# Pair counts of a graph kernel: one-hots compared two tiles side by side, against lane numbers kept in a PSUM bank

## The reference

```
edge_index = stack([src, dst])                       # 400,000 edges, sorted by dst
x = layernorm(x + L0(x, edge_index, ...))            # attention over the edges, softmax by src
x = layernorm(x + L1(x, node_vec1, ...))             # two masked sums over the edges
x = layernorm(x + L2(x, edge_weight, edge_attr, ...))# radial weights, messages, sum by dst
x = layernorm(x + L3(x, edge_index, ...))            # two graph convolutions
```

## Time and profile before

| | |
|---|---|
| median of 3 runs | 20,091.51 us (20,090.82 to 20,093.43) |
| profiled execution, span from the first to the last instruction | 25,995.0 us |
| time outside the span | none is given |
| busy in the span | PE 9,853; PEld 7,351; DVE 16,714; ACT 6,289; POOL 13,430 us |
| mean granted PE clock | 0.611 of 2.4 GHz |
| pair counts, first comparison to the copy of bank 0 | 1401.9 to 2067.9 us of the span |

### The profile page before, as it was taken

One profiled execution on the slowest core, in us unless ns is written; L12 is line 12 of the kernel. 1 busy time (PEld: TensorE's weight loads), 2 busy tenths in 40 slices (PEclk: granted clock), 3 DMA queues, 4 the chain that ended last, 5 costly groups with the idle time before them and its releaser, 6 DMA issues.

```text
span 25995.0 us, 290953 instructions
## 1 busy us (share of the span) xinstructions
PE 9853.2 (38%) x63545; PEld 7350.7 (28%) x63546; DVE 16714.1 (64%) x23622; ACT 6288.5 (24%) x13799; POOL 13429.9 (52%) x14067
## 2 busy tenths in 40 slices
PE   0131000000000006765225666666666666324422
PEld 0131000000000006664223444444444444313421
DVE  9898574547344438888555666666666677555555
ACT  0002121112111105543002333333333345201400
POOL 0187676667777760000664555555555552363165
PEclk6555555555555559985556777777777776555555
DMA  1133434441000001116222000000000006424623
GB/s 14 25 33 27 29 31 29 29 29 13 6 6 6 6 15 48 41 52 227 69 69 18 9 10 9 9 9 9 9 9 9 9 10 144 137 64 87 205 65 61
DMA packets 1751558, 1095.98 MB, mean 42 GB/s; under 512 B 1217323, under 2 KB 1658124, under 8 KB 1750028
## 3 DMA queue, kind: packets, MB, share of 16 engines
q0 software_dynamic: 454272, 412.11, 13.3%
q1 hardware_dynamic: 1089532, 417.46, 6.8%
q10 hardware_dynamic: 207632, 265.14, 3.3%
HBM read 700.94 MB, written 391.12 MB: 42 GB/s over the span
## 4 chain that ended last, share of the span: by engine, by line
DVE 31%; another core or an unknown queue 21%; issue 17%; DVEq 12%; PE 11%; ACT 4%; DMA 2%; ACTq 1%; POOL 0%; SPq 0%; POOLq 0%
PE banks L1423 5%; DVE arena L1768 5%; DVE arena L1767 4%; DVE red L2523 4%; DVEq L2201 3%; DVE hot L2196 2%; DVE arena L1740 2%; DVE arena L2207 2%; DVE srcs L2516 2%; PE banks L1365 2%; PE banks L1410 2%; DVEq L498 1%; DVE arena L1585 1%; DVEq L2261 1%
## 5 line engine op out<-in xcount | busy, mean ns | idle before, releaser
L804 POOL DMA_INDIRECT srcs<-spread,nbx x2808 | 2653.2, 945 | 5691.9 <-issue 3372.8
L782 POOL DMA_INDIRECT gat<-tab,nbr x3328 | 3455.0, 1038 | 2537.8 <-issue 1271.9
L1423 PE MATMUL banks<-w2rows,dsts 128*128 128x384 f32 x6656 | 3443.8, 660 | 1030.2 <-DVE srcs L2516 699.0
L782 POOL DMA_INDIRECT gat<-tab,pay x3328 | 3161.6, 950 | 1077.4 <-issue 892.0
L748 POOL DMA_INDIRECT pay<-records,nbr x2560 | 2746.2, 1073 | 843.1 <-issue 827.1
L1208 PE MATMUL banks<-ident,arena 128*128 128x128 f32 x2240 | 436.2, 379 | 7154.4 <-DVE arena L1768 2837.8
L909 ACT COPY banks<-arena 128x1024 f32<-128x1024 f32 (+1 forms) x1508 | 1318.6, 875 | 6430.8 <-issue 2701.9
L2511 DVE TENSOR_TENSOR srcs<-banks,g_s 128x512 f32<-128x512 f32 x1664 | 1146.1, 689 | 2252.6 <-remote 1505.1
L1208 PEld LDWEIGHTS banks<-ident,arena 128*128 128x128 f32 x2240 | 400.7, 204 | 7190.5 <-DVE arena L1768 2844.2
L2523 DVE TENSOR_REDUCE red<-srcs 128x160 f32<-128x2560 f32 x832 | 2346.2, 2820 | 75.6
L1279 PE MATMUL banks<-srcs,hot 128*128 128x96 bf16 (+1 forms) x11232 | 1169.8, 281 | 3175.7 <-DVE hot L2196 2136.8
(11 more groups left out here) (392 smaller groups left out, 22029.8 us busy)
## 6 DMA issues: line engine op xcount, KB each, us to landing
spread<-srcs SPq DMA_DIRECT2D x936, 192.0 KB, 2.9
dsts<-key_rows SPq DMA_DIRECT2D x234, 512.0 KB, 4.1
spread<-srcs ACTq DMA_DIRECT2D x468, 204.0 KB, 2.4
staged<-gat SPq DMA_DIRECT2D x416, 148.0 KB
gat<-staged ACTq DMA_DIRECT2D x416, 148.0 KB, 2.1
dsts<-key_rows ACTq DMA_DIRECT2D x117, 512.0 KB, 4.3
gat<-tab,nbr POOLq DMA_INDIRECT x3328
gat<-tab,pay POOLq DMA_INDIRECT x3328
```

Source lines behind the costliest of these rows:

```text
L782: pool.indirect_dma_start(out=gatv(s, GC[pas])[:, t, :], out_offset=None, in_=TAB[pas], in_offset=bass.IndirectOffsetOnAxis(ap=row, axis=0 ...
L804: pool.indirect_dma_start(out=chunk_rows(s, c)[:, q, :], out_offset=None, in_=rows, in_offset=bass.IndirectOffsetOnAxis(ap=nbx[:, r, s * X ...
L1423: last = t_.matmul(bank[1 + 2 * (p % 2) + h][:, 0:384], hid_rows[:, s % 2, 2 * p + h, :], w2rows[:, :], start=True, stop=True)
```

## The change

The one-hots of the pair counts take the form that attention's have.

- `pair_hot` is seen as [tile pair, lane, tile of the pair] instead of [tile, lane]. The two bf16 of a pair alternate, and PE's two operands step by 4 bytes.
- The lane numbers are staged once in `pair_lanes` as bf16 pairs and copied to PSUM bank 5. The comparison's first operand is that bank, its second the keys of two tiles.
- The keys get one more column, -1, so that the last step has an even number of tiles: 6 instead of 5. PE runs 3126 matmuls.

```diff
+        pair_lanes = acc[:, 3400:3400 + P]
+        pair_hot = [[acc[...].bitcast(BF16)
+                     .rearrange("p (t w q) -> p t w q", w=W, q=2) for k in range(2)] for b in range(2)]
...
-                        mm = t_.matmul(bank[0][0:W, 0:W], pair_hot[b][0][:, t, :], pair_hot[b][1][:, t, :],
+                        mm = t_.matmul(bank[0][0:W, 0:W], pair_hot[b][0][:, t // 2, :, t % 2], pair_hot[b][1][:, t // 2, :, t % 2],
...
-                step(full, 1, TE % HT, last=True)
+                step(full, 1, TE % HT + TE % 2, last=True)
...
-                    v.tensor_copy(out_, whole)
+                    v.tensor_copy(out_[:, 0:TE], whole)
+                    v.memset(out_[:, TE:TE + TE % 2], -1.0)
                     dve.drain()
+                v.tensor_copy(pair_lanes.bitcast(BF16).rearrange("p (n q) -> p n q", q=2),
+                              iota[:, :].rearrange("p (n a) -> p n a", a=1).to_broadcast([P, P, 2]))
+                dve.drain()
+                v.tensor_copy(bank[5][:, 0:P], pair_lanes)
+                dve.drain()
...
                         last = v.tensor_tensor(
-                            pair_hot[b][k][:, 0:tiles, :],
-                            iotaw.rearrange("p (a w) -> p a w", a=1).to_broadcast([P, tiles, W]),
-                            ends[:, bass.ds(n * HT, tiles)].rearrange("p (t a) -> p t a", a=1).to_broadcast([P, tiles, W]),
+                            pair_hot[b][k][:, 0:tiles // 2, :, :],
+                            lane_pairs[:, 0:W, :].rearrange("p (a w) q -> p a w q", a=1).to_broadcast([P, tiles // 2, W, 2]),
+                            ends[:, bass.ds(n * HT, tiles)].rearrange("p (t a q) -> p t a q", a=1, q=2).to_broadcast([P, tiles // 2, W, 2]),
                             ALU.is_equal)
```

More of the change, by code:

```diff
@@ L199, in resnorm_gnn_kernel @@
         hot = sb("hot", [P, 2, TPS, P])
[L201 to L204, removed]
+        own_w = acc[:, 0:(TE + 1) // 2].bitcast(BF16)
+        nbr_w = acc[:, 1600:1600 + (TE + 1) // 2].bitcast(BF16)
+        pair_lanes = acc[:, 3400:3400 + P]
+        pair_hot = [[acc[:, 8192 + (2 * b + k) * 784:8192 + (2 * b + k + 1) * 784].bitcast(BF16)
+                     .rearrange("p (t w q) -> p t w q", w=W, q=2) for k in range(2)] for b in range(2)]
         high_w = acc[:, 0:DGROUPS * DIGITS // 2].bitcast(BF16)
@@ L1596, in pair_counts @@
                     step(i * 2 + 2, 0, HT)
-                step(full, 1, TE % HT)
+                step(full, 1, TE % HT + TE % 2)
                 dve.wait_ge(pairs_used, full + 3)
```

## The result

The changed kernel takes 19,897.6 us (median of 4 runs, 19,879.7 to 19,904.9), the kernel before 20,091.6 beside it. The ratio is 0.9901, with an interval of 0.9889 to 0.9913: 194 us faster, where 308 were forecast, and 38 us above the upper end of the range. The direction was right and the size was not.

A forecast was written before the change was run, and what follows sets the result against it. It took DVE to bound the pair counts and everything behind to wait for it: 195 steps x (3.40 - 1.82) = 308 us, so 20,091.5 - 308 = 19,784 us, own range 19,770 to 19,800, full range 19,765 to 19,860.

The forecast's parts named there:

- The comparison: Pair counts on DVE: one comparison of 1568 elements falls from 1781 to 967 ns.
- The step: Pair counts, two comparisons and 16 matmuls: 3.40 us falls to 1.78 to 1.84, taken as 1.82; 195 steps save 308 us.
- the forecast's loop through PE's burst: Pair counts: comparisons, PE's burst and buffer reuse form a loop of 3.69 us over two steps, 1.84 a step.
- rival A: Pair counts: PE's moving operand at half speed, 172 ns a matmul, makes PE the bound; 19,965 us; chance 0.08 in any degree.
- The stage: Pair counts, first comparison to L1607: some 357 us where it was 666.
- POOL in the stage: POOL's gathers beside the pair counts: about 284 at 0.94 us fit in the stage, not 391.
- DVE's landmarks: Sorts, ACT's load and attention after the pair counts: each about 308 us earlier, distances between them unchanged.
- The failing step: From pair counts to the end: everything behind them moves earlier by what the counts save, 308 us.
- slack of 3,080 us: POOL's gathers for the maxima end at 6046 and ACT first loads their result at 9126.7, so POOL is not awaited.
- some 158 us earlier: POOL's gather chain ends 310 - 152 = 158 us earlier than now; said to change POOL's count, not the sum.
- Rival C: Behind the pair counts: a wait for POOL or a DMA takes the gain back, 20,091 us at worst; chance 0.03.
- rival D: Pair counts: DVE's packed comparison must wait for POOL's running gather, 51 us slower, 20,142 us; chance 0.03.

The follow-up runs named there:

- experiment 3: Kernel before with its slow f32 comparison, only the f32 lane numbers read from a PSUM bank: 19,901.6 us, ratio 0.9910.
- experiment 1: Kernel before, unchanged, profiled once more because the first profile was far longer than its timed runs: 20,107.3 us, span 20,104.6.
- experiment 5: Changed kernel with 96 record gathers moved behind the later pass's gathers, but the slow f32 comparison with lanes in PSUM: 19,889.0 us, ratio 0.9905.
- experiments 2: Changed kernel with the lane pairs left in SBUF, so the fast comparison has two SBUF inputs: 19,979.2 us, ratio 0.9954.
- experiment 6: Changed kernel with 96 record gathers moved and the packed comparison also in the source-node counts, their lanes in SBUF: 19,759.0 us, ratio 0.9839.
- experiment 7: Changed kernel with 96 record gathers moved and packed source-node counts, the lanes of those counts in PSUM: 19,744.4 us, ratio 0.9834.
- experiment 4: Changed kernel with 96 of POOL's 2560 early record gathers moved behind the gathers of the pass after attention: 19,779.7 us, ratio 0.9850.

## Why the prediction was wrong

Point by point, by its own steps.

- **The comparison**: forecast 967 ns, measured 966 to 967. Right. By the Trainium skill, "VectorE: DVE Perf Modes", section on the TRN2 errata, it would have been an estimated 942; the row is 25 ns dearer, and a PSUM source costs nothing extra here (967 ns with either place in the fast form; 1777 in experiment 3 against 1784 with SBUF lanes in experiment 1).
- **The step**: forecast 1.82 us of 1.78 to 1.84. From the first to the last comparison it is (1757.1 - 1408.3)/195.5 = 1.784, DVE alone. At the lower level two bursts in a row start 1.76 and 1.86 us apart, 1.81 a step, near the forecast's loop through PE's burst (1.84). For over half of the stage PE had the upper level.
- **PE's operands with a step of 4 bytes** (rival A): 16 matmuls in 1.57 us at the lower level, as before. Free. That was right, but partly by luck: the ground for the moving operand was the f32 burst of L1279, 119 ns a matmul at the upper level, set against 86 ns at the lower one. At the stage's own level the same 16 matmuls take 3.88 us (the row below), (3.88 - 0.56)/15 = 221 ns, which is 163 for 98 columns and speaks for the rival's 172.

```profile
9819.17 3.88 PE L1279 MATMUL banks<-msg,hot 128*128 128x133 f32 x16 [1.24 <-DVE msg L2265]
```

- **The stage**: forecast some 357 us, measured 351 (1408.3 to the copy at 1759.0) from 666. Right, six us better.
- **POOL in the stage**: forecast 284 gathers at 0.94, measured 284 at 0.95. Right.
- **DVE's landmarks** "about 308 earlier": the arrival at the pass after attention is 308.5 earlier. Right.
- **The failing step** is the one that joins DVE's chain to the end: "So what the counts save should move everything behind them by as much." It rests on the slack of 3,080 us between the earlier trace rows and on POOL's 9635.5 against DVE's 12,311.5. Both are distances between two engines in an execution that was 5,903 us too long. I had noted that excess, asked only whether it lay in the stage, and then read slack from other places of the same trace. In an unstretched execution (experiment 1) POOL's last record gather comes 260 us after DVE's arrival. So before and after the change the pass is begun by POOL.
- **What the gain is**: POOL's chain, with a term that the prediction called without effect on the sum. There the 391 gathers of the stage come 666/391 = 1.703 us apart, and without a second SBUF input 662/530 = 1.249 (experiment 3). 391 x (1.703 - 1.249) = 178 us. The prediction put this at "some 158 us earlier", from 1.42 us a gather in the stretched sorts; measured is 9045.7 - 8852.7 = 193.0. Of the 15 us between 178 and 193, the plain gathers explain about all: 947 ns in the one execution and 944 in the other, over 5,888 of them 18 us. Experiment 5 bears it out, with the slow comparison and gathers of 944 ns: POOL's first series lasts 4340.3 us there and 4530.8 in experiment 1, 190 less, of which 10 are the 3 ns of 3,328 gathers; 180 are left. The measured 194 has an interval of 175 to 223 us, so it agrees with 178, and its nearness to 193.2 is in part chance.
- **Rival C**, the gain taken back behind the stage by a wait for POOL, got 0.03 and is what happened to 114 of the 308 us. My ground against it was that same slack. Its other half was missing too: it had the wait taking the gain back whole, and did not ask what the change does to POOL's own chain.

The rows at hand were enough to doubt it. In the earlier trace rows DVE is busy for 3,785 of the 7,035 us of the sorts. If the 5,903 us too many lie where engines stand idle, attention can start 7035 - 3785 = 3,250 us earlier in a timed run, at 6,560, and DVE arrive at the pass at 12,311.5 - 3,250 = 9,062, ahead of POOL's 9,636. POOL's gathers run one behind the other (944 ns and 0.30 between) with little wait, so 9,636 looks as if it could shrink only a little. It shrank by 590, to 9045.7, and DVE's arrival still more, to 8786.0: the rows gave the order of the two chains, not the 260 us between them. With POOL last the forecast would have been POOL's term: 20,091.5 - 158 to 178, that is 19,914 to 19,934. Those are 16 to 36 us above the measured time, in place of 114 below.

By the Trainium skill, "SBUF — State Buffer", section Who interferes with whom, a DVE instruction with two SBUF inputs contends with a GpSimd instruction that reads SBUF, and one with a single SBUF input does not. The gathers read their row numbers (`nbr`) from SBUF, and experiments 2 and 3 agree on both halves (1485 and 946 ns a gather). The prediction cited the rule and set it aside as changing "POOL's count and not the sum"; it was the sum.

## What to carry over

Slack between two engines is a distance in one execution. When the profiled one is much longer than the timed ones, first find the stretch that holds the excess, take it out, and only then say which chain comes last. Judge a change to one engine by what it does for the engines beside it: here the DVE instruction became 814 ns shorter, and once its constant operand lay in PSUM, where it left POOL free, a gain from the shorter length is not shown any more. Once the last chain is relieved, part of that gain comes back (experiment 5: some 37 us by the landmarks, more where attention runs at a lower clock), so try the two together.

## What the runs showed of the hardware that I had not expected

- A profiled execution can be 29% longer than timed ones (25,995 against 20,091 us) with its DVE instructions at their usual lengths (1781 against 1784 ns for the comparison). The excess lay mostly in idle time, 3,125 us of it in the sorts of DVE, while attention (1,685 against 1,688 us from first to last comparison) was untouched and POOL's gathers up to the pass took 590 us longer (the records' median was 1091 ns against 947; up to 9,105 they ran beside the sorts, which end at 5,980 in experiment 1). It turned round which chain came last.
- POOL's indirect DMAs beside a DVE comparison with two SBUF inputs keep step with DVE: one gather for each comparison of 1.78 us, 1.70 apart, and with comparisons of 0.97 us one for every two, 1.78 apart. DVE did not pay (1784 against 1777 ns without a second SBUF input). A gather's row is 0.94 us long when it is not held up and 1.41 and 1.49 in the two cases.
- Beside POOL's tensor operations DVE does pay: the comparison of 1.08 us took up to 1.93 with its lanes in SBUF (experiment 6) and never over 1.08 with them in PSUM (experiment 7). That is rival D's mechanism, in another place and with another kind of POOL instruction.
- PE took weights and a moving operand whose bf16 elements lie 4 bytes apart at no cost, at the lower level.
- Attention's PE clock differed between executions of these kernels: 1.00 granted and 1,687 us long in experiment 4, 0.93 and 1,749 us in experiment 5, with nothing changed in attention. Only where DVE's chain came last did it reach the time.
